# The last sequence's feed-forward written out by hand at the end of a run of windowed layers

## The reference

```
x = x + 0.5 * sign_ffn(layernorm(x))
x = x + rope_attention(layernorm(x))
x = x + 0.5 * sign_ffn(layernorm(x))
x = x + 0.5 * windowed(layernorm(x))       # run 0 of windowed_layers
x = x + delta_memory(layernorm(x))
x = x + 0.5 * windowed(layernorm(x))       # run 1 of windowed_layers

def windowed(x):                            # 6 layers, window 32, 16 heads of 64
    for i in range(6):
        x = attn_layer(shift_tokens(x), ...) + x
        x = ffn_layer(shift_tokens(x), ...) + x
    return x

def ffn_layer(x, g, bln, W1, b1, W2, b2):
    xn = (x - mean) / sqrt(var + 1e-5) * g + bln
    a, gate = split(xn @ W1 + b1)           # 341 wide each, padded to 3 blocks of 128
    return a * gelu(gate) @ W2 + b2
```

## Time and profile before

| what | value |
|---|---|
| median of 3 runs | 4434.81 us (4418.97 to 4439.37) |
| the profiled execution's own time | 4437.24 us |
| its span | 4435.4 us |
| mean granted clock of PE | 0.935 of full |
| PE busy | 4056.5 us (91%) |
| DVE busy | 3024.3 us (68%) |
| POOL busy | 2739.5 us (62%) |
| ACT busy | 2112.4 us (48%) |

### The profile page before, as it was taken

How to read it: one execution, slowest core, us unless ns; L and a number is a source line. 1 busy time by engine, 2 the same in 40 slices (tenths; PEclk the granted TensorE clock), 3 DMA queues, 4 the chain that set the end, 5 groups by cost and what they waited for, 6 DMA issues and landing times. The chain is left out here.

```text
span 4435.4 us, 129901 instructions
## 1 busy us (share of the span) xinstructions
PE 4056.5 (91%) x56144; PEld 2602.4 (59%) x56144; DVE 3024.3 (68%) x3465; ACT 2112.4 (48%) x2625; POOL 2739.5 (62%) x3481
## 2 busy tenths in 40 slices
PE   8999889999999999999867776999999999999996
PEld 4333456666666666666536663666666666666663
DVE  1575167878778788788534334787877787877873
ACT  2455245555555555555421112555555555555552
POOL 0000088787878788878514224878877788787771
PEclk9899989999999999999966557999999999999997
DMA  0000100000000000000000001000000000000000
GB/s 18 1 1 1 48 11 11 11 17 11 2 17 11 17 11 2 7 2 2 2 8 4 4 4 58 11 11 2 17 12 17 12 2 17 11 7 2 2 2 10
DMA packets 14119, 46.30 MB, mean 10 GB/s; under 512 B 3808, under 2 KB 6240, under 8 KB 11744
## 3 DMA queue, kind: packets, MB, share of 16 engines
q1 hardware_dynamic: 13536, 37.83, 2.4%
HBM read 36.78 MB, written 1.05 MB: 9 GB/s over the span
## 5 line engine op out<-in xcount | busy, mean ns | idle before, releaser
L706 POOL TENSOR_TENSOR w_qk<-w_turned 128x1024 f32<-128x1024 f32 x384 | 906.8, 2362 | 149.3 <-DVE w_turned L586 147.0
L250 PE MATMUL w_ps_qk<-w_w_qk,ZT 128*128 128x512 f32 x1536 | 764.2, 621 | 75.6 <-DVE w_turned L586 53.1
L294 PE MATMUL w_ps_y<-w_px,w_w_vo 128*128 128x128 f32 x6144 | 786.8, 276 | 2.5 <-DVE ZT L682 2.5
L294 PEld LDWEIGHTS w_ps_y<-w_px,w_w_vo 128*128 128x128 f32 x6144 | 742.6, 192 | 77.8 <-issue 74.0
L735 POOL TENSOR_TENSOR w_qk<-w_qk,w_inv_norm 128x1024 f32<-128x1024 f32 x384 | 722.7, 1904 | 0.0
L476 ACT ACTIVATE w_squares<-w_ps_qk 128x1024 f32<-128x1024 f32 x384 | 393.4, 1024 | 661.7 <-PE w_ps_qk L250 661.7
L581 DVE TENSOR_TENSOR w_turned<-w_ps_qk,w_rot_l 128x1024 f32<-128x1024 f32 x384 | 467.3, 1217 | 232.9 <-ACT w_squares L476 207.8
L743 POOL TENSOR_TENSOR w_probs<-w_probs,w_row_inv 128x1024 f32<-128x1024 f32 x192 | 365.3, 1903 | 362.6 <-DVE w_row_inv L613 361.9
L250 PEld LDWEIGHTS w_ps_qk<-w_w_qk,ZT 128*128 128x128 f32 x1536 | 280.4, 195 | 407.4 <-issue 304.5
L480 ACT ACTIVATE w_px<-w_ps_w 128x1024 f32<-128x1024 f32 x384 | 379.0, 1021 | 209.1 <-PE w_ps_w L286 209.1
L586 DVE TENSOR_TENSOR w_turned<-w_ps_qk,w_rot_l 128x1024 f32<-128x1024 f32 x384 | 466.1, 1214 | 0.0
(11 more groups left out here) (247 smaller groups left out, 6106.3 us busy)
## 6 DMA issues: line engine op xcount, KB each, us to landing
w_w_qk<-in_w_qk SPq DMA_DIRECT2D x12, 1024.0 KB, 4.8
w_w_vT<-in_w_vT SPq DMA_DIRECT2D x12, 512.0 KB, 3.6
w_w_o<-in_w_o SPq DMA_DIRECT2D x12, 512.0 KB, 5.0
w_w<-in_w SPq DMA_DIRECT2D x12, 384.0 KB, 3.1
w_w<-in_w SPq DMA_DIRECT2D x12, 192.0 KB, 3.1
XT<-in_x SPq DMA_DIRECT2D x1, 1024.0 KB, 4.8
w_rot<-in_rot SPq DMA_DIRECT2D x2, 512.0 KB, 5.7
out<-XT SPq DMA_DIRECT2D x1, 1024.0 KB, 3.9
```

Of the source, the lines that this page charges most:

```text
L250: last = nc.tensor.matmul(ps_qk[:, c, :], Z[:, T.col:T.col + P], w_qk[:, T.parity, cols], start=True, stop=True)
L294: last = nc.tensor.matmul(ps_y[:, D.t * P:(D.t + 1) * P].rearrange("p (w q) -> p w q", q=WIN), w_vo[:, D.parity, h, p, :], px[:, D.odd, :, ...
L706: nc.gpsimd.tensor_tensor(qk[:, T.odd, which, :], turned[:, which, 0, :], turned[:, which, 1, :], ALU.add).then_inc(pool_add, 1)
```

## The change

Steps 100 to 104 are no longer walked (`ALL_STEPS` goes from `TOTAL + 9` to `TOTAL + 4`). Each engine then calls a function `finish`, which writes out what they held for the last sequence `f`, with `down` of the one before it (`prev`):

- the intermediate results go to banks that the attention has left: centred values, variance and spread values to `ps_w` 0, 1 and 2, the three gate blocks to `ps_w` 0 to 2, the three up blocks to `ps_w` 3 and the two banks of `ps_qk`;
- ACT applies Gelu with its bias to each gate block straight from PSUM, three instructions in place of four; the Exp call of step 99 is dropped;
- `down` of `prev` comes on PE behind the variance, and its residual on DVE ahead of `normal`;
- in step 99 the attention's residual of the last sequence (`residual`, L682 before) comes ahead of the last `hidden` of sequence 22, no longer after it;
- half sums are done for each sequence, three of them in `finish` behind `normal`, the fourth behind the last `feed`; the function `half_sum` and its barrier are gone;
- in run 1 SP stores each sequence as its half sum is done, 256 KB at a time, in place of one transfer of 1024 KB;
- `d_w` and `d_tab` are issued in the block of `layer_norm` 4;
- `broadcast` uses `nc.tensor.transpose` in place of `nc.tensor.matmul` with the identity, in all sequences of both runs.

```diff
-ALL_STEPS = TOTAL + 9
+ALL_STEPS = TOTAL + 4
...
+        final_up = lambda i: ps_w[:, 3, :] if i == 0 else ps_qk[:, i - 1, :]
...
+                for b in range(BATCH):
+                    sp.wait_ge(added, BATCH * run + b + 1)
+                    sp.dma_start(out[:, b * SEQ:(b + 1) * SEQ], XT[:, b * SEQ:(b + 1) * SEQ]).then_inc(stored, 16)
...
-                    last = nc.tensor.matmul(ps_f[:, t * P:(t + 1) * P], rstd[:, t:t + 1].broadcast_to([P, P]),
-                                            ident[:], start=True, stop=True, skip_group_check=True)
+                    last = nc.tensor.transpose(ps_f[:, t * P:(t + 1) * P], rstd[:, t:t + 1].broadcast_to([P, P]), ident[:])
...
+            def finish(f, prev):          # PE
+                pe.wait_ge(dve_y, f.m + 1)
+                nc.tensor.matmul(ps_w[:, 0, :], centre[:], Z[:, f.col:f.col + SEQ], start=True, stop=True).then_inc(pe_cen, 1)
+                pe.wait_ge(act_cen, f.m + 1)
+                for t in range(TILES):
+                    last = nc.tensor.matmul(ps_w[:, 1, t:t + 1], xn_sq[:, t * P:(t + 1) * P], mean_col[:],
+                                            start=True, stop=True, skip_group_check=True)
+                last.then_inc(pe_var, 1)
+                pe.wait_ge(dve_hid, prev.m * FFB + FFB)
+                for i in range(FFB):
+                    last = nc.tensor.matmul(ps_f[:], w_2[:, prev.parity, i, :], hid[:, i, :], start=i == 0, stop=i == FFB - 1)
+                last.then_inc(pe_down, 1)
+                pe.wait_ge(pool_rstd, f.m + 1)
+                for t in range(TILES):
+                    last = nc.tensor.transpose(ps_w[:, 2, t * P:(t + 1) * P], rstd[:, t:t + 1].broadcast_to([P, P]), ident[:])
+                last.then_inc(pe_bc, 1)
+                pe.wait_ge(dve_xn, f.m + 1)
+                for i in range(FFB):
+                    nc.tensor.matmul(ps_w[:, i, :], w_1[:, f.parity, FFB + i, :], xn[:], start=True,
+                                     stop=True).then_inc(pe_gate, 1)
+                for i in range(FFB):
+                    nc.tensor.matmul(final_up(i), w_1[:, f.parity, i, :], xn[:], start=True, stop=True).then_inc(pe_up, 1)
+                pe.wait_ge(dve_z, prev.m + 1)
+                for i in range(FFB):
+                    pe.wait_ge(dve_hid, f.m * FFB + i + 1)
+                    last = nc.tensor.matmul(ps_f[:], w_2[:, f.parity, i, :], hid[:, i, :], start=i == 0, stop=i == FFB - 1)
+                last.then_inc(pe_down, 1)
...
-                if s.up:
+                if s.up and s.k < TOTAL + 3:
                     nc.scalar.activation(warm[:], warm_in[:], ACT.Exp)
...
+            def finish(f):                # ACT
+                act.wait_ge(pe_cen, f.m + 1)
+                nc.scalar.activation(xn_sq[:], ps_w[:, 0, :], ACT.Square)
+                nc.scalar.activation(xn[:], ps_w[:, 0, :], ACT.Copy).then_inc(act_cen, 1)
...
+                for i in range(FFB):
+                    act.wait_ge(pe_gate, f.m * FFB + i + 1)
+                    nc.scalar.activation(hid[:, i, :], ps_w[:, i, :], ACT.Gelu,
+                                         bias=b_h[:, f.parity, FFB + i:FFB + i + 1]).then_inc(act_gate, 1)
...
+            def half_sum(b):              # DVE
+                dve.wait_ge(dve_z, M0 + (DEPTH - 1) * BATCH + b + 1)
+                at = EDGE + SPAN * b
+                for half, col in ((lower, at), (upper, at + 1)):
+                    x = XT[half, b * SEQ:(b + 1) * SEQ]
+                    last = nc.vector.scalar_tensor_tensor(x, Z[half, col:col + SEQ], 0.5, x, ALU.mult, ALU.add)
+                last.then_inc(added, 1)
...
+            def finish(f, prev):          # DVE
...
+                feed(prev)
+                dve.wait_ge(pe_bc, f.m + 1)
+                nc.vector.scalar_tensor_tensor(xn[:], xn[:], vec[:, f.parity, 0:1], ps_w[:, 2, :],
+                                               ALU.mult, ALU.mult).then_inc(dve_xn, 1)
+                for b in range(BATCH - 1):
+                    half_sum(b)
+                for i in range(FFB):
+                    dve.wait_ge(pe_up, f.m * FFB + i + 1)
+                    dve.wait_ge(act_gate, f.m * FFB + i + 1)
+                    nc.vector.scalar_tensor_tensor(hid[:, i, :], final_up(i), b_h[:, f.parity, i:i + 1], hid[:, i, :],
+                                                   ALU.add, ALU.mult).then_inc(dve_hid, 1)
+                feed(f)
+                half_sum(BATCH - 1)
...
             walk(pool, run, step)
+            invert_roots(final_chain, final)
```

More of the change, by code:

```diff
@@ L136, in __call__, with windowed_layers @@
         return self.held[name]
-def windowed_layers(nc, run, sem, Z, consts, dram):
+def windowed_layers(nc, run, sem, Z, consts, dram, XT, added, store=None):
     tag = f"w{run}"
@@ L144, in windowed_layers @@
     N0, M0, L0 = run * TOTAL, run * DEPTH * BATCH, run * DEPTH
+    final, before_final = Rows(run, 0, DEPTH * BATCH - 1), Rows(run, 0, DEPTH * BATCH - 2)
+    final_chain = Step(run, 0, TOTAL + 4).chain
     ctx = ExitStack()
@@ L557, in step @@
                     tokens_out(B)
+            def finish(f):
+                act.wait_ge(pe_cen, f.m + 1)
+                nc.scalar.activation(xn_sq[:], ps_w[:, 0, :], ACT.Square)
+                nc.scalar.activation(xn[:], ps_w[:, 0, :], ACT.Copy).then_inc(act_cen, 1)
+                act.wait_ge(dve_floor, final_chain + 1)
+                act.wait_ge(pool_inv, final_chain)
+                nc.scalar.activation(bits[:], floor[:].bitcast(I32), ACT.Identity, bias=seed[:, 0:1],
+                                     scale=-0.5).then_inc(act_guess, 1)
+                act.wait_ge(pe_down, f.m)
+                for i in range(FFB):
+                    act.wait_ge(pe_gate, f.m * FFB + i + 1)
+                    nc.scalar.activation(hid[:, i, :], ps_w[:, i, :], ACT.Gelu,
+                                         bias=b_h[:, f.parity, FFB + i:FFB + i + 1]).then_inc(act_gate, 1)
+                nc.scalar.activation(warm[:], warm_in[:], ACT.Copy).then_inc(act_gelu, 1)
             act.wait_ge(edged, run + 1)
             walk(act, run, step)
+            finish(final)
         @block.vector
@@ L591, in sum_squares, with residual, feed @@
                                      .rearrange("p (h d) -> p h d", d=DH), AXX).then_inc(dve_ss, 1)
+            def residual(f, D):
+                dve.wait_ge(pe_y, D.n + 1)
+                for half, at in ((lower, f.col), (upper, f.col + 1)):
+                    rows = Z[half, at:at + SEQ]
+                    last = nc.vector.tensor_tensor(rows, ps_y[half, :], rows, ALU.add)
+                last.then_inc(dve_y, 1)
+            def feed(f):
+                dve.wait_ge(pe_down, f.m + 1)
+                for half, at in ((lower, f.col), (upper, f.col + 1)):
+                    rows = Z[half, at:at + SEQ]
+                    last = nc.vector.scalar_tensor_tensor(rows, ps_f[half, :], vec[half, f.parity, VEC - 1:VEC], rows,
+                                                          ALU.add, ALU.add)
+                last.then_inc(dve_z, 1)
+            def half_sum(b):
[5 more added lines that the diff above has]
+                last.then_inc(added, 1)
             def normal(f):
@@ L618, in step @@
                 if s.down:
[L619 to L625, removed]
+                    feed(s.down)
                 if C:
@@ L674, in step @@
                     normal(s.bc)
+                if s.y and s.k == TOTAL + 3:
+                    residual(s.y, D)
                 if s.up:
                     hidden(s.up, 2)
[L677 to L683, removed]
+                if s.y and s.k < TOTAL + 3:
+                    residual(s.y, D)
+            def finish(f, prev):
+                dve.wait_ge(pe_var, f.m + 1)
+                nc.vector.tensor_scalar(sumsq[:, 2 * HEADS:NORMS, 0], ps_w[:, 1, 0:TILES], EPS, 0.5,
+                                        ALU.add, ALU.mult).then_inc(dve_var, 1)
+                dve.wait_ge(dve_var, f.m + 1)
+                dve.wait_ge(pool_inv, final_chain)
+                nc.vector.tensor_reduce(floor[:], sumsq[:], AXX, ALU.max).then_inc(dve_floor, 1)
+                feed(prev)
[11 more added lines that the diff above has]
+                half_sum(BATCH - 1)
             walk(dve, run, step)
-            dve.wait_ge(dve_z, M0 + DEPTH * BATCH)
+            finish(final, before_final)
+            dve.wait_ge(added, BATCH * run + BATCH)
         @block.gpsimd
@@ L821, with layer_norm @@
 BLK = FF0 // P
-def layer_norm(nc, run, sem, src, dst, consts, shifted=False):
+def layer_norm(nc, run, sem, src, dst, consts, shifted=False, fetch=()):
     tag, base = f"n{run}", run * BATCH
@@ L839, in layer_norm, with _ @@
         cols = [slice(b * SEQ, (b + 1) * SEQ) for b in range(BATCH)]
+        @block.sync
+        def _(sp):
+            for into, given, fetched in fetch:
+                sp.dma_start(into[:], given).then_inc(fetched, 16)
         @block.tensor
@@ L2095, in _ @@
```

(6 more changed lines are left out.)

4 lines of the change are left out of this document (added).

## The result

| | median of four runs | lowest to highest |
|---|---|---|
| before | 4430.24 us | 4418.97 to 4439.37 |
| changed | 4353.75 us | 4351.62 to 4366.80 |

The ratio is 0.9834, with a 95% interval of 0.981 to 0.9858. That is 76.5 us less by the medians and 63 to 84 us by the interval. The forecast was 4366, with a range of 4348 to 4402. It took its 69.5 us off a median of 4434.81; with the fourth run that median is 4430.24, so 4.6 of the 12 us between forecast and result lie in the kernel before.

A forecast was written before the change was run, and what follows sets the result against it. PE's own stream was taken to bound the steady part. Tail gains of 25.4 and 24.4 us plus 19.7 for transposes made 69.5 off 4437.24, giving 4367.7, stated as a median of 4366; range 4348 to 4402.

The forecast's parts named there:

- The bound: Steady part of the windowed layers: PE's own stream sets the time, busy 194 of 200 us at full clock.
- Transposes, 19.7: 46 broadcasts in the steady part as transposes: 0.53 us less PE each, 19.7 us gained in all, bounds 0 and 24.4.
- Tail up to `normal`, 6.8: Each tail, step 99 to the start of `normal`: gain 6.8 us, from 4.9 to 7.3 without a table load.
- `normal` to the last product, 13.2: Each tail, `normal` to the last product's end: nine blocks back to back, 23.5 us becoming 10.3, gain 13.2.
- The 2.3 us: Nine blocks in each tail: middle loss while the clock comes back, added to 8.0 us at full clock.
- the bounds: Gain from `normal` to the last product: 7.7 us at half clock throughout, 15.5 at the upper end.
- Rival 2: Both tails: PE stays at half clock through `finish`, 2 x 5.5 us more, giving 4377; chance 0.17.
- Rival 3: Both tails: the nine blocks are each held by their reader, third term 0, giving 4392; chance 0.04 alone.
- Half sums, store, loads, 5.4 and 4.4: End of each tail: 5.4 us gained in the second pass, 4.4 in the first; the moved loads are free.
- the 0.5 of my sum: Start of `layer_norm` 4: of 1.6 us lost to half clock, 0.5 was counted as gained.

The follow-up runs named there:

- run 1: Second of the two passes inside each execution, not a follow-up kernel: its walk to the tail took 1671.9 us before, 1672.0 changed.
- run 0: First of the two passes inside each execution, not a follow-up kernel: its walk to the tail took 1674.4 us before, 1650.9 changed.
- the first profile: Profile of the changed kernel from its first measurement against the kernel before: span 4351.8 us; median of four runs 4353.75 us, ratio 0.9834.
- the second: Second profile of the changed kernel, run once more with nothing altered: ratio 0.9822 to the kernel before, median 4348.84 us.

## Why the prediction was right

**The bound.** PE's stream sets the steady part: 4 rows less of it (1.16 became 0.65) shorten the step by 0.50 or 0.45.

**Transposes, 19.7.** Measured 22 by the medians of the steps, 24 by the walks less their stalls. Before the scores 0.50 for a forecast 0.53. After them 0.45 for 0.27: the 0.21 to L273 is what I had worked out, and the rest I had missed. It shows later in that step, where PE's rows close up. In step 38 of run 0, counted from the maximum of step 37, L273 comes 0.21 earlier (3.26 for 3.47), the second pair of projection products 0.35 (8.40 for 8.75) and the gather 0.45 (10.21 for 10.66). By the runs the edit is worth 27 to 30. With transposes alone the last broadcast, in the tails, gives 4.7 of what is above 22. The stretch behind `layer_norm` 4, in code that the edit does not touch, was 4.7 to 5.0 shorter in its profile; why is open. I had no term for a change of layout.

**Tail up to `normal`, 6.8.** Measured 7.4 and 7.0 in the first profile, 7.0 and 7.4 in the second. The broadcast, which I had at half clock and 1.1, took 0.65 at full in both runs; where `down` of 22 ran slowly, its residual took some of that back. The order in step 99 and the clock both matter, by the experiment with the residual last. No table load stood before the guess: ACT's Identity ran with Gelu's table as the Trainium skill says in ScalarE: Activation LUTs, "Table sets: the hidden batching unit".

**`normal` to the last product, 13.2.** Measured 12.5 to 15.5 from `normal` to the last residual: 24.4 became 8.8 in two of the four tails that were profiled, 10.4 and 11.9 in the others. The 2.3 us that I had added for a start at half clock was a middle value that came in none of them: the blocks took 8.0, 9.6 or 11.1, not 10.3. Over all eight profiles with this `finish`, ten of 16 tails took 8.8, with the clock up from the first block, five some 10.5 and one 11.9. Which clock a tail gets I had not foreseen; the bounds covered it. Rival 2, half clock throughout, did not come: the row of nine blocks brought the clock up where it was down. Rival 3, blocks held one by one, did not come either; with their waits put back they took 18.3 with the clock up at first, and 23.7 at half clock, near the 24.4 of before, as that rival says.

**Half sums, store, loads, 5.4 and 4.4.** Measured 5.9 and 3.7. The store of 256 KB landed in 2.1, not 2.7. The clock at the start of `layer_norm` 4 goes either way: half in the first profile (six rows in 4.51), full in the second (2.81), where all of the 1.6 was gained and not the 0.5 of my sum. It lies in the stretch behind the tail. With the code shifted by 32 and 64 waits it was full as well, in the other profiles not.

**Not in the sum.** The unlike walks come from where PE's code lies: run 1's walk gained as much by transposes as run 0's and lost it to 23 stalls. Over the layouts tried the two walks together came to 9 to 29 us less than in the two profiles of before, around the 22 of the rows. The 6.5 us behind `layer_norm` 4, in code that the change does not touch but for the place of two loads, are of open cause. The loads are not it: with them issued early again (half sums behind barriers) the stretch took 437.5. Layout alone is not shown either: two executions of the changed kernel took 435.9 and 430.7, with as much idle PE put down to nothing (46.4 and 47.2, gaps from 0.3 us on), and only 1.7 of the 5.2 between them is the clock at the start. So a part of the 83.6 in the profiles is no merit of the prediction, whose terms give 69.5.

The rule that full clock does not engage for transposes (the Trainium skill, TensorE: Matmul & The Clock Gate, Part 4) did not bear here: with 46 broadcasts more in transposes the granted clock from 1400 to 1600 was 1.00, as before, and the steps became shorter.

## What to carry to other kernels

A tail that belongs to the last tile alone deserves code of its own: give every intermediate a free bank, put older work beneath the latency chain, and let reductions and stores follow each piece. A float32 product with the identity, in a stream that PE bounds, is worth writing as a transpose, and the smallest piece counts if it stands before something DVE is waiting for. When a change moves code, compare at least two layouts before reading 0.3% into it, and don't read a term off one copy of a stage that exists twice, nor off one profile where the clock can go either way.

## What the runs showed that I had not expected

- PE's stalls behind nothing visible, 0.6 to 4.3 us each and 42 to 60 us in all of the steady part, keep their places from execution to execution of a program and move when its code is shifted. In four profiles each of them went with an instruction transfer. Five layouts of the same work (as it is, and shifted by 32 to 128 waits) spread from 0.9802 to 0.9844 in ratio.
- The clock of `finish` was not the same from one execution to the next: in run 0 of the first profile `down` of 22 ran at full clock (2.82 us) and the nine blocks began at half, in run 1 `down` took 4.52 and they ran at full throughout. That is worth up to 3.1 us a tail (8.8 against 11.9).
- A one-column float32 product is not small: 80 rows took 17.2 us at PE's lower clock, 0.215 each, with 128 columns of weights loaded for each.
